# GpSimd's lookups in the build stage of a two-layer graph network: from the fifth edge group on, each waits for a count of one-hots

## The reference

```
h = relu(layernorm(x));  x = x + L0(h)
h = relu(layernorm(x));  x = x + L1(h)

L0: two GIN steps   agg = segment_sum(h[src], dst); h = mlp2(h + agg)
L1: y = mlp3(h)[src]; z = segment_sum(y, dst); out = mlp3(concat(h, z))
```

## Time and profile before

| what | value |
|---|---|
| median of three runs | 937.94 us (937.82 to 939.57) |
| span of the profiled execution | 976.2 us |
| the profiled execution's time outside its span | not given on the page |
| `build` in that span | 0 to 422 us |
| `net` in that span | 422 to 976 us |
| TensorE, VectorE, GpSimd busy | 91%, 72%, 42% of the span |

### The profile page before, as it was taken

How to read it: one execution, slowest core, us unless ns; L and a number is a source line. 1 busy time by engine, 2 the same in 40 slices (tenths; PEclk the granted TensorE clock), 3 DMA queues, 4 the chain that set the end, 5 groups by cost and what they waited for, 6 DMA issues and landing times.

```text
span 976.2 us, 25210 instructions
## 1 busy us (share of the span) xinstructions
PE 889.8 (91%) x11282; PEld 722.6 (74%) x11282; DVE 699.2 (72%) x656; ACT 479.9 (49%) x573; POOL 407.2 (42%) x281
## 2 busy tenths in 40 slices
PE   0577999859999999989999999999999999999996
PEld 0246988749999999967777777777777866777774
DVE  7784999829999999757456655555545686677773
ACT  2643645335544555346454554554555365555551
POOL 5874388870880000030663546760001143444450
PEclk9967999878999999999999999999999999999998
DMA  3022434414434334441444434444442367788871
GB/s 108 18 84 80 137 102 130 133 39 134 136 103 140 124 123 131 135 147 58 132 132 132 119 94 128 129 117 119 113 128 85 93 197 222 212 242 239 239 218 48
DMA packets 81857, 126.86 MB, mean 130 GB/s; under 512 B 10288, under 2 KB 58544, under 8 KB 81616
## 3 DMA queue, kind: packets, MB, share of 16 engines
q1 hardware_dynamic: 78608, 121.98, 41.7%
q0 software_dynamic: 3136, 3.22, 1.5%
HBM read 84.22 MB, written 40.94 MB: 128 GB/s over the span
## 4 chain that ended last, share of the span: by engine, by line
PE 49%; DVE 4%; ACT 2%; issue 1%; DMA 0%; POOL 0%; DVEq 0%; POOLq 0%; ACTq 0%
PE net_ps_hi L1271 14%; PE net_ps_lo L1271 14%; PE net_ps_hi L1288 7%; PE net_ps_lo L1288 6%; PE net_ps_mt L1214 4%; PE net_ps_ft L1214 2%; ACT net_wide L1110 1%; DVE net_wide L833 1%; PE net_ps_check L1306 1%; DVE hT L926 1%; DVE hT L921 1%; DVE net_first L933 1%; PE net_ps_mt L1318 0%; DMA net_raw<-edge_counts 0%; POOL net_wide L879 0%
## 5 line engine op out<-in xcount | busy, mean ns | idle before, releaser
L1271 PE MATMUL net_ps_hi<-net_wide,net_first 128*128 128x512 f32 (+1 forms) x637 | 248.5, 394 | 1.3 <-POOL net_wide L879 1.3
L338 DVE TENSOR_TENSOR build_hot_lo<-build_grid_lo,build_keys_t 128x4096 bf16<-128x4096 bf16 x100 | 225.3, 2284 | 26.7 <-PE build_ps_cnt L569 14.3
L1271 PE MATMUL net_ps_lo<-net_wide,net_first 128*128 128x512 f32 (+1 forms) x637 | 240.8, 382 | 0.0
L589 PE MATMUL build_ps_out<-build_parts_pad,build_cnts 128*128 128x195 bf16 x2401 | 234.9, 256 | 3.4 <-issue 1.9
L833 DVE CAST net_wide<-net_raw 128x3584 fp32r<-128x3584 uint8 (+1 forms) x90 | 201.2, 2243 | 44.2 <-PE net_ps_lo L1288 16.9
L1110 ACT ACTIVATE net_wide<-net_raw 128x3584 fp32r<-128x3584 uint8 (+1 forms) x64 | 193.6, 3025 | 78.9 <-PE net_ps_lo L1271 44.8
L456 ACT ACTIVATE build_cnts<-build_ps_cnt 128x980 uint16<-128x980 f32 (+3 forms) x176 | 150.5, 901 | 160.4 <-PE build_ps_cnt L569 130.5
L589 PEld LDWEIGHTS build_ps_out<-build_parts_pad,build_cnts 128*128 128x128 fp8e4 x2401 | 212.8, 101 | 11.3 <-issue 5.4
L259 POOL DMA_INDIRECT build_edges<-in_edges,build_start_i x49 | 114.6, 2339 | 70.2 <-DVE build_start_i L322 56.5
L1271 PEld LDWEIGHTS net_ps_hi<-net_wide,net_first 128*128 128x128 f32 x637 | 119.8, 188 | 31.9 <-issue 7.0
L1271 PEld LDWEIGHTS net_ps_lo<-net_wide,net_first 128*128 128x128 f32 x637 | 119.9, 188 | 24.7 <-issue 2.6
(11 more groups left out here) (171 smaller groups left out, 708.4 us busy)
## 6 DMA issues: line engine op xcount, KB each, us to landing
net_raw<-edge_counts SPq DMA_DIRECT2D x168, 448.0 KB, 3.7
edge_counts<-build_cnts SPq DMA_DIRECT2D x168, 224.0 KB
xres<-in_x SPq DMA_DIRECT2D x1, 1568.0 KB, 6.8
net_raw<-edge_counts SPq DMA_DIRECT2D x14, 112.0 KB, 2.0
out<-xres SPq DMA_DIRECT2D x12, 128.0 KB, 4.1
build_rows<-in_dst_rows,build_row_i POOLq DMA_INDIRECT x49
build_edges<-in_edges,build_start_i POOLq DMA_INDIRECT x49, 4.3
edge_counts<-build_cnts SPq DMA_DIRECT2D x7, 112.0 KB
```

What stands on the lines that cost most here:

```text
L338: return v.tensor_tensor(hot.rearrange("p c (k t) -> p c k t", t=2), grid[:, :].rearrange("p (k t) -> p k t", t=2)[:, None, :, :].broadcas ...
L589: last = nc.tensor.matmul(to, cnts[u % A_RING][:, w % 2, c, :], parts66[:, c, :, with_check], start=(c == 0), stop=False)
L1271: last = nc.tensor.matmul(ps[(b + 1) % 2][:, 0:n * P], first[:, c, lo:lo + H], expanded[e % WIDE_RING][:, 0:n, k, :], start=(c == 0), stop ...
```

## The change

The lookups of edge groups 4 to 8 and of row groups 6 to 8 get a wait each on the hot count. `in_pace` waits for `first + int(apart * i)`, where i is the lookup's place in its group: edge groups 4, 5, 6 and 7 wait for counts from 9, 17, 33 and 48 on, rising by one, edge group 8 from 56 on, rising by two; row group 6 from 13 on, two lookups at each count, row groups 7 and 8 from 25 and 41 on, rising by one. `ROWS_BEHIND` moves row group 6 from behind edge group 5 to behind edge group 4, and row group 7 stays behind edge group 5. Each quarter then has one lookup in turn from count 17 to 55, with a gap of none or a few counts between groups. No other engine's instructions change.

```diff
-ROWS_BEHIND = {2: (4,), 3: (5,), 5: (6, 7), 6: (8,)}
+ROWS_BEHIND = {2: (4,), 3: (5,), 4: (6,), 5: (7,), 6: (8,)}
+EDGES_AFTER = {4: (9, 1), 5: (17, 1), 6: (33, 1), 7: (48, 1), 8: (56, 2)}
+ROWS_AFTER = {6: (13, 0.5), 7: (25, 1), 8: (41, 1)}
...
+                def in_pace(after, g, i):
+                    if g in after:
+                        first, apart = after[g]
+                        pool.wait_ge(hot_ready, first + int(apart * i))
+
                 def gather_rows(g, lo, hi):
                     for w in range(lo, hi):
+                        in_pace(ROWS_AFTER, g, w - lo)
                         nc.gpsimd.indirect_dma_start(rows[:, w, :], None, a["dst_rows"],
...
                     pool.wait_ge(starts_known, g + 1)
                     for w in range(lo, hi):
+                        in_pace(EDGES_AFTER, g, w - lo)
                         nc.gpsimd.indirect_dma_start(edges[:, w, :, :].rearrange("p e k -> p (e k)"), None, a["edges"],
```

## The result

The changed kernel takes 941.66 us, median of five runs (940.17 to 943.78). The kernel before took 937.82 us beside it (five runs, 935.73 to 939.57). The ratio is 1.0049, 95% interval 1.0032 to 1.0065: slower by 0.5%, about 4 us. 932 us and "faster" were predicted. The direction is wrong; the time lies in the range of 920 to 952.

The account below looks back on a forecast made before the run. The prediction took VectorE's one-hots to set the pace, with lookups disturbing TensorE in two stretches. 7 us gained less 1 charged gave 6: 937.9 - 6 = 932 us, range 920 to 952, chance of faster 0.42.

Parts of the forecast that it names:

- What the profiled execution says of the runs: Whole run: span 38.3 us over the median, at most 25 us of it profiler cost in the net stage's large matmul.
- times of a third in the runs: Build stage: a share of 0.32 of the 22.4 us saved in a profile counts in timed runs, 7 us.
- the holes: Build stage, 75 to 92 and 181 to 221 us: VectorE waits while lookups disturb TensorE's counting, 37.8 us together.
- nothing to win: Rival: the 181 to 221 us stall is the profiler's, runs are already paced by VectorE, 938 us stays; chance 0.27.
- The late hole goes: Build stage, 181 to 221 us: paced lookups remove VectorE's 23.8 us of waits, less 1.4, so 22.4 us in a profile.
- Row group 6 moved up: Build stage, counts 13 to 16: eight lookups placed where GpSimd was idle, charged 1 us, bounds 0 and 6.5.
- the early hole: Build stage, 75 to 92 us: 14.0 us of VectorE's waits, which the change was to leave as they are.
- Five quarters, 15.9 us, against a landing of 4.3: Edge group 5: issued at counts 17 to 24, needed at 29, so its edges land in time.
- Lookups stand 3 us apart: Sign that the forecast is right, build stage: one lookup per quarter pair, 3.17 us; build stage ending near 400 us.
- Held lookups: Rival: paced lookups get stuck between VectorE's one-hots for 10 us or more, edges come late, 946 to 953 us; chance 0.23.
- ScalarE and row group 8: Pair 11: ScalarE may wait 0 to 4 us for these rows, charged 0 because PSUM buffers and VectorE's ring cover it.
- The reading of the loop: Build stage: lookups disturb TensorE, VectorE idles, lookups then come at 1.25 us intervals and disturb more; 37.8 us of waits.

Follow-up runs that it names:

- before_again: The kernel before, unchanged, profiled a second time: 937.11 us with the profiler, 937.54 us without (median of 29 runs).
- edges2_early: Kernel before with GpSimd's two tag multiplications and half of row group 3 behind edge group 2: 977.55 us, ratio 1.0080 to the kernel before (0.9997 to 1.0164).
- after_c: The changed kernel repeated on a chip with gaps: 957.64 us, ratio 0.9951 to the kernel before (970.54 us there).
- rows6_half: Kernel before with four of row group 6's eight lookups ahead of edge group 5, no waits: 968.17 us, ratio 1.0034 to the kernel before (0.9973 to 1.0094).
- pace_rows: Kernel before plus the change's waits on row groups 6 to 8 alone, on a chip with gaps: 950.30 us, ratio 0.9854 to the kernel before.
- pace_only_b: Repeat on a second chip of the changed kernel's waits with the order of before: 938.78 us, ratio 1.0020 to the kernel before (1.0007 to 1.0034).
- half_paced: Changed kernel with only four of row group 6's lookups ahead of edge group 5 and the rows' counts shifted: 936.79 us, ratio 1.0001 to the kernel before.
- pace_only: The changed kernel's waits with the order of groups of the kernel before: 939.80 us, ratio 1.0014 to the kernel before (0.9997 to 1.0030).
- after_again: The changed kernel repeated on a second chip without gaps: 943.00 us, ratio 1.0072 to the kernel before (1.0058 to 1.0085).
- order_only: The changed kernel's order of groups without any of its waits: 941.25 us, ratio 1.0036 to the kernel before (1.0021 to 1.0051).
- order_only_b: Repeat on a second chip of the changed order without waits: 940.88 us, ratio 1.0042 to the kernel before (1.0028 to 1.0055).
- tags_later: Kernel before with GpSimd's two tag multiplications moved behind edge group 2, on a chip with gaps: 973.95 us, ratio 1.0066 to the kernel before.
- pace_edges: Kernel before plus the change's waits on edge groups alone, on a chip with gaps: 962.76 us, ratio 1.0034 to the kernel before (0.9994 to 1.0074).

## Why the prediction was wrong

**"What the profiled execution says of the runs", and "times of a third in the runs": this step failed.** The 38.3 us between span and median were taken to be up to 25 us of profiler cost in the large matmul and at least 13 us of the holes. The profiler costs nothing that can be seen: in `before_again` the profiled execution took 937.11 us, within the spread of the runs without it, and its span was 1.8 us less, as in every other run. So the first profiled execution took about 978.0 us by estimate (976.2 + 1.8), 40.1 more than the median, and the holes make up 37.8 of it. All of them were missing in the runs, and the share was 0, not 0.32. The term of 7 us is 0. The rival "nothing to win" had the share right, by the near agreement of 38.3 and 37.8 and the spread of 0.2%; I named both and gave it 0.27. Its reason, that the hole is the profiler's, is wrong: `before_again` has the profiler and no hole. The 226.5 ns of a large matmul were no sign of the profiler either: in `before_again` ten steps of it take 598.00 - 595.73 = 2.27 us, 227 ns each. The Trainium skill's 215.7 ns (TensorE: Matmul & The Clock Gate, "Wait — 56ns, not 53.3ns?") is thus not what this fp32r matmul, with a weight load each, reaches in a profiled execution: with 1911 of them the 10.8 ns would be 20.6 us, and the profiled execution is no longer than the others.

**"The late hole goes": not tested by the result, and not settled where there is a hole.** 22.4 us were expected in a profiled execution. On the first chip with gaps, `edges2_early` against `after_c`, VectorE's busy time in 181 to 221 us rose from 16.61 to 38.13, 21.5 us, and the medians fell by 13 us, 58% of 22.4. The comparison's interval leaves that chip open (0.9893 to 1.0009), and `rows6_half` and `pace_rows` show that part of it, or all, may be luck of the execution. On the second chip with gaps the waits win, by a mechanism that isn't shown.

**"Row group 6 moved up", 1 us with bounds 0 and 6.5: this step failed too, mis-sized and for the wrong reason.** With a share of 0 it is the term that makes the kernel slower. The step looked at TensorE's share, 0.18 us a lookup, and at an idle GpSimd, 26.50 us of it. The charge on TensorE doesn't hold without the holes: in `before_again` TensorE is busy 56.00 of 56 us beside 24 lookups. The idle time goes with the early hole: on the chips without gaps GpSimd has none there, and eight lookups at 18.6 / 8 = 2.3 us (99.57 to 118.19) push eight edges back by 18.6 us. The order alone costs 1.0036 and 1.0042, 3.4 and 3.9 us, where 1 was charged, and VectorE's wait is 3.0 to 3.7 us in the five traces that have this order on a chip without gaps.

**"Five quarters, 15.9 us, against a landing of 4.3": failed with it.** The slack was counted from count 24, as if the waits set the time of issue. They were no limit: GpSimd was behind its counts until about 180 us. The last edge was issued at 136.48, 0.7 us after VectorE wanted it; 3.0 us to its landing gives the wait of 3.70. "Lookups stand 3 us apart" fell with it: until 137 us they stand 2.3 us apart. The build stage ended at 385.6 us, not near 400, as the early hole was missing as well.

**Held lookups, the rival for "slower": wrong mechanism, right sign and symptom.** VectorE does wait for edges ahead of group 5's keys, as it said, but no lookup of the changed kernel takes more than 3.95 us. That the time lies in the range of 920 to 952 is luck: its upper part was there for held lookups. The longest are paced ones after an idle time, as at 255.62 us:

```profile
255.62 3.95 POOL L268 DMA_INDIRECT build_edges<-in_edges,build_start_i  x1 [1.65 <-DVE build_hot_lo L347]
```

Holds of 10.55 us came back at the old place on chips with gaps (`pace_rows`, 113.91), in four of the five kernels there that have no waits on the edges and in none that has them. By the Trainium skill (SBUF — State Buffer, "Who interferes with whom") whoever is first has the shared port for the whole instruction; the page says so of VectorE's two-port modes. The 3.95 us are 3.0 over the 0.94 us of an unhindered lookup, within VectorE's longest instruction of 3.49 us; the 10.55 us aren't.

**ScalarE and row group 8: 0 to 4 us foreseen, charged at 0.** It waits 6.67 us, and the build stage ends no later for it. The charge was right.

**What the waits alone cost, and where.** The changed kernel loses 0.49 and 0.72%. The order explains 0.36 to 0.42%. The waits alone cost 0.14 (interval with 0 in it) and 0.20%. In their two traces the build stage ends 0.1 and 0.9 us later than before's, and the net stage, where nothing was edited, is 2.7 and 4.1 us longer (555.8 and 557.2 us against 553.1). TensorE's granted clock shows where. The stretch in which the net stage begins, and eight of its matmuls in order of time, in `before_again`, then the same in `pace_only_b`:

```profile
384.00:392.00 8.00, 7.28 (x53) 5.25 (x52) 5.27 (x7) 5.32 (x11) 6.22 (x6) 1.00 0.74 274
...
385.33 1.16 PE L1214 MATMUL net_ps_hi<-w_L_gnn_W,net_hid 128*128 128x128 f32 x8
```

```profile
384.00:392.00 8.00, 7.49 (x43) 5.53 (x44) 2.89 (x4) 4.31 (x8) 6.13 (x6) 0.79 0.74 265
...
385.99 2.07 PE L1223 MATMUL net_ps_hi<-w_L_gnn_W,net_hid 128*128 128x128 f32 x8
```

In both traces of the waits alone the clock is 0.79 from 384 to 392 us, a mean between its two levels of 1.2 and 2.4 GHz, and 0.97 from 725 to 780 us; in `before_again` and `half_paced` it is 1.00 in both stretches. An estimate from these figures is 0.21 x 8 + 0.03 x 55 = 3.3 us. The other executions agree. The span times the missing share of the clock is 15.9 us on average over the twelve of `pace_only` and over the twelve of `pace_only_b`, against 13.8 and 14.0 us over the 29 and 23 of before beside them and 13.6 in `half_paced`. The differences are 2.2 and 2.0 us (standard error 0.9 each); the medians differ by 2.3 and 2.0. For the changed kernel (`after_again`) it is 17.3 us, so part of its 0.72% is clock as well. This sum is no price where TensorE waits for VectorE anyway: `order_only` has 16.6.

**What stays open.** Why the clock falls there isn't shown: from 380 to 384 us TensorE is busy 2.44 of 4 us in `before_again` and in `pace_only_b` alike, `half_paced` has waits and no such fall, and `order_only_b` has no waits and the second one (0.97 from 725 to 780 us). Nor is it shown why some chips have the gaps. The reading of the loop has one small count against it: on a chip without gaps three lookups at 1.25 us intervals (137.73 to 140.23 in the changed kernel) leave TensorE without a gap until 140.64.

## What to carry to other kernels

Compare the profiled execution's time with the runs before you read a stall from it: where it is 4% longer, the stall belongs to that execution until a second one shows it, and slack read beside it can be false as well. Before a transfer is put ahead of another in one queue, count the issue times of everything in it from where the queue really is, not from the waits that are meant to hold it. If lookups are to be moved ahead of others, move only as many as the others' slack bears: `half_paced`, with four ahead instead of eight, costs nothing where the changed kernel loses 0.7%. Where a stage that wasn't edited gets longer, compare the granted clock of its stretches.

## What the runs showed of the hardware

The kernel before took 936.7 and 937.5 us on two chips, and 959.7, 970.5 and 977.3 us in three comparisons on two others. On the latter TensorE had gaps of up to 1.2 us (1.9 in `tags_later`) that waited for nothing the profile shows, 12 to 31 us in all from 50 to 400 us in the kernels without waits, while GpSimd issued lookups. On the first two the one trace of the kernel before had none in that stretch with the same lookups, and no other trace more than one in the counting (0.7 us the longest). The granted clock in the third and fourth slice was lower in most traces with gaps (6 and 7 tenths in `after_c` and `pace_rows`, 8 and 9 in `before_again`), but not in all: `pace_edges` has 7 and 9, as the changed kernel's first trace without gaps. The row of `pace_rows`:

```profile
PEclk9967999999999999999999999999999999999998
```

A lookup by GpSimd took 0.94 us with VectorE idle (136.48 in the changed kernel), and mostly 1.90 to 3.10 us beside full one-hots, 2.3 us from start to start over eight of them, so VectorE's load sets how far behind GpSimd falls.

The same eight matmuls took 1.16 us in one execution and 2.07 us in another, where the granted clock was down; two such falls in the net stage come to 3.3 us by the estimate above, where it was 2.7 and 4.1 us longer.
